# A stack of graph layers on one core: one of eight gather slots of the attention read densely on TensorE, the leaky relu's linear part added by VectorE

## The reference, cut to what matters

```python
def _gatv2(x, src, dst, Wl, Wr, att, bias):
    xl = (x @ Wl).reshape(-1, H, C)
    xr = (x @ Wr).reshape(-1, H, C)
    e = jax.nn.leaky_relu(xl[src] + xr[dst], 0.2)
    logits = jnp.einsum('ehc,hc->eh', e, att)
    m = jax.ops.segment_max(logits, dst, num_segments=N_NODES)
    p = jnp.exp(logits - m[dst])
    denom = jax.ops.segment_sum(p, dst, num_segments=N_NODES)
    alpha = p / denom[dst]
    out = jax.ops.segment_sum(alpha[:, :, None] * xl[src], dst, num_segments=N_NODES)
    return out.mean(axis=1) + bias
```

## Time and profile before

| What | Value |
|---|---|
| Median of 3 runs | 6472.8 us (6467.22 to 6487.99) |
| Profiled execution: its time | 6470.45 us |
| Its span, first to last instruction | 6468.7 us |
| PE busy | 5462.8 us, 84%, 47565 matmuls |
| PE weight loads | 3535.7 us, 55% |
| DVE busy | 3216.3 us, 50% |
| ACT busy | 1959.8 us, 30% |
| POOL busy | 4227.3 us, 65% |
| Mean granted clock of PE | 0.92 of full speed |
| DMA | 626.97 MB, mean 97 GB/s |
| Chain that ended last, by engine | PE 40%, POOL 29%, issue 15%, DVE 9% |

### The profile page before, as it was taken

The page is one execution under the profiler, slowest core; times in us unless marked ns, Lnnn a source line. Parts: engine busy times, 40 slices in busy tenths (PEclk is TensorE's granted clock), DMA queues, the critical chain, the costliest instruction groups (busy, mean ns, idle before and its releaser), DMA issues.

```text
span 6468.7 us, 138175 instructions
## 1 busy us (share of the span) xinstructions
PE 5462.8 (84%) x47565; PEld 3535.7 (55%) x47565; DVE 3216.3 (50%) x5767; ACT 1959.8 (30%) x3916; POOL 4227.3 (65%) x4383
## 2 busy tenths in 40 slices
PE   1888888868886888689999986899999679999995
PEld 1666666667775777535455544354444444455553
DVE  8222323266567555535555555355555624555555
ACT  0333334345551000033333321333333123333330
POOL 0777777657775777477777742777777147777770
PEclk8899989879997999789999996999999879999997
DMA  1444444323332332234444431444444224444441
GB/s 36 113 114 113 113 113 113 102 72 83 78 83 66 83 83 77 54 87 119 117 121 121 120 94 38 104 120 117 121 121 118 65 56 116 120 119 121 119 117 32
DMA packets 645340, 626.97 MB, mean 97 GB/s; under 512 B 366244, under 2 KB 447915, under 8 KB 644779
## 3 DMA queue, kind: packets, MB, share of 16 engines
q1 hardware_dynamic: 498218, 437.16, 22.1%
q0 software_dynamic: 140352, 181.29, 14.6%
q10 hardware_dynamic: 6208, 1.37, 0.1%
HBM read 530.77 MB, written 88.55 MB: 96 GB/s over the span
## 4 chain that ended last, share of the span: by engine, by line
PE 40%; POOL 29%; issue 15%; DVE 9%; ACT 2%; DMA 2%; DVEq 1%; POOLq 0%
POOL rows L340 29%; PE ps L761 11%; PE ps L877 10%; PE ps L848 4%; PE ps L776 4%; PE ps L865 2%; PE ps L856 2%; DMA rows<-table,idx 2%; DVE region L1326 1%; DVE acc L1442 1%; PE ps L947 1%; PE ps L833 1%; PE ps L788 1%; DVE region L1034 1%; PE ps L963 1%
## 5 line engine op out<-in xcount | busy, mean ns | idle before, releaser
L340 POOL DMA_INDIRECT rows<-table,idx x3328 | 3231.9, 971 | 1556.8 <-issue 1108.3
L877 PE MATMUL ps<-region,hot 128*128 128x272 f32 x4992 | 1320.0, 408 | 92.2 <-DVE acc L1442 87.9
L877 PEld LDWEIGHTS ps<-region,hot 128*128 128x128 f32 x4992 | 910.9, 192 | 507.9 <-issue 335.8
L573 ACT ACTIVATE region<-ps 128x512 f32<-128x512 f32 x1248 | 677.4, 595 | 1681.9 <-PE ps L848 1681.9
L1442 DVE TENSOR_TENSOR acc<-acc,ps 128x272 f32 x1248 | 545.2, 437 | 1195.6 <-PE ps L877 1088.5
L1432 DVE TENSOR_TENSOR region<-ps,region 128x1056 f32<-128x1056 f32 x624 | 781.7, 1253 | 64.8 <-issue 53.7
L761 PE MATMUL ps<-hot,region 128*128 128x192 bf16 (+1 forms) x7488 | 773.0, 266 | 13.2 <-issue 9.6
L848 PE MATMUL ps<-xT,wcat 64*128 64x512 f32 x2496 | 721.9, 655 | 7.4 <-ACT region L573 4.9
L761 PEld LDWEIGHTS ps<-hot,region 128*128 128x128 bf16 x7488 | 701.9, 105 | 40.8 <-issue 9.9
L352 POOL DMA_INDIRECT rows<-table,idx x528 | 502.6, 952 | 270.5 <-issue 160.3
L865 PE MATMUL ps<-region,attblk 128*32 128x512 f32 x2496 | 667.5, 614 | 0.0
(11 more groups left out here) (264 smaller groups left out, 5880.0 us busy)
## 6 DMA issues: line engine op xcount, KB each, us to landing
hot<-hot_dram SPq DMA_DIRECT2D x624, 256.0 KB
turned<-turned_dram SPq DMA_DIRECT2D x624, 128.0 KB
rows<-table,idx POOLq DMA_INDIRECT x3856
hot_dram<-hot SPq DMA_DIRECT2D x104, 512.0 KB
xwin<-table SPq DMA_DIRECT2D x1664, 24.0 KB
region<-hot_dram SPq DMA_DIRECT2D x78, 512.0 KB
turned_dram<-turned SPq DMA_DIRECT2D x104, 256.0 KB
region<-r_dram SPq DMA_DIRECT2D x78, 256.0 KB
```

The costliest lines, as they stand in the source:

```text
L340: pool.indirect_dma_start(rows[:, b, j, :], None, table, bass.IndirectOffsetOnAxis(ap=idx[:, s:s + 1], axis=0)).then_inc(gathered[b], 16)
L573: act.activation(rz[:, 2 * t + side, :], ps[:, Z + side, :], ACT.Relu).then_inc(rz_made, 1)
L877: mm = pe.matmul(ps[:, AG + i, 0:PC + H], hot[:, b, 4 * side + 2 * i + j, :], px[b][:, 4 * side + 2 * i + j, :], start=(j == 0), stop=(j = ...
```

## The change

1. *One slot of eight.* POOL gathers the first seven slots of a group. The eighth (side 1, j = 3) is read densely: SP's `numbers_for` loads a chunk's eight source numbers, broadcast, one DMA a chunk; DVE's `stationary_one` makes the four one-hot matrices of eight slots at once (four instructions a chunk, in phases 3 and 4); PE's `read_one(u + 2)` runs 12 bf16 matmuls into the free columns 272 to 495 of the first sums bank, behind `z_half(u, 0)`; DVE's `pick_one(u + 2)` multiplies by a mask and sums the candidates into `xs`, two instructions; `rows_in` turns that slot by one float32 matmul in place of three bf16 ones.
2. *The linear part.* `linear` and `linblk` go. ACT's relu scales by 0.8, and DVE's new `leaky` computes rz = 0.2 z + rz for 128x1024 values, reading z from PSUM, twice a step. `z_half` and the logits now wait for DVE.
3. *The logits.* All four products of a group are issued together at the step's end, each into 32 output partitions of its own; within a chunk the partitions are now ordered by head, then by group. The flags, the maxima's tiles (`exchange` copies in four parts), `fall` and `fdiag` (64 rows) follow this order.
4. *New orders and waits.* DVE in an ordinary step: `weigh` side 0, `leaky` 0, `weigh` side 1, `add` side 0, pick, `leaky` 1, `add` side 1. `rows_in` waits for the pick. `sums_half(k, 1)` waits for the pick of u + 2, since both use one bank. `read_one` waits for the adds of k - 1.
5. *Layer start.* The table's bf16 parts are copied to `tabC`, and the four masks of the first chunk are made. The self products are summed in seven parts inside the loop of 25 (four windows each), no longer by one instruction behind it. DVE's first two picks follow the clearing of `acc`.
6. *Before the attention.* `linblk`, the sums of weights that filled it and the scaling of `attblk` go; the masks `spanhot` of the runs of 512 nodes (13 small comparisons) and `headsel` are added; the flags are spread by 16 instructions of half the size.

```diff
@@ pool_gathers @@
-                slots = range(8 * g, 8 * g + 8) if pas == 0 else piece_slots(g)
+                slots = range(8 * g, 8 * g + 8) if pas == 0 else piece_slots(g)[0:7]
@@ sp_attention @@
+            def numbers_for(c):
+                if c >= CHUNKS:
+                    return
+                at = l * CHUNKS + c
+                if at >= 2:
+                    sp.wait_ge(bt1_made, FOLD * (at - 1))
+                first = CHUNK * c + CHUNK // 2 + PIECE - 1
+                sp.dma_start(rline1[at % 2].rearrange("p (n e) -> p n e", n=8),
+                             r_dram.rearrange("a (f e) -> (a f) e", f=2)[first:first + 29:4, :].partition_broadcast(P)
+                             ).then_inc(r1_in[at % 2], 16)
...
             for u in range(G + LAG):
+                if u % 8 == 5:
+                    numbers_for(u // 8 + 2)
@@ act_attention @@
                 for side in range(2):
-                    act.activation(rz[:, 2 * t + side, :], ps[:, Z + side, :], ACT.Relu).then_inc(rz_made, 1)
+                    act.activation(rz[:, 2 * t + side, :], ps[:, Z + side, :], ACT.Relu, scale=0.8).then_inc(relu_made, 1)
@@ pe_attention @@
+            def logits(g):
                 n = g % 8
+                pe.wait_ge(rz_made, 2 * (l * G + g) + 2)
...
+                for side in range(2):
+                    for t in range(2):
+                        q = 64 * side + 32 * t
+                        pe.matmul(ps[q:q + 32, LG, :], attblk[l][:, t, 7 - n:7 - n + 32], rz[:, 2 * t + side, :],
+                                  start=(n == 0), stop=(n == 7), skip_group_check=True).then_inc(l_summed, 1)
+
+            def read_one(g):
...
+                pe.wait_ge(bt1_made, FOLD * (at + 1))
+                if l * G + g > 0:
+                    pe.wait_ge(one_picked, l * G + g)
+                for k in range(FOLD):
+                    cols = len(range(k, W, FOLD)) * C
+                    for s in range(3):
+                        mm = pe.matmul(ps[:, AG, 272:272 + cols], bt1[at % 2][:, k, n, :],
+                                       tabC[:, k::FOLD, s * C:(s + 1) * C], start=(k == 0 and s == 0),
+                                       stop=(k == FOLD - 1 and s == 2), skip_group_check=True)
+                mm.then_inc(one_read, 1)
...
                 pe.wait_ge(att_added, 4 * (l * G + k) + 2 * side)
+                if side == 1 or k + LAG + 2 >= G:
+                    pe.wait_ge(one_picked, l * G + min(k + LAG + 3, G))
...
                 if u < G:
                     z_half(u, 0)
+                if u + 2 < G:
+                    if k > 0:
+                        pe.wait_ge(att_added, 4 * (l * G + k))
+                    read_one(u + 2)
...
                 if u < G:
-                    linear(u)
                     z_half(u, 1)
-                    logits_half(u, 0)
...
                 if u < G:
-                    logits_half(u, 1)
+                    logits(u)
@@ vector @@
+            def stationary_one(l, c, k):
...
+                v.tensor_scalar(bt1[at % 2][:, k, :, :].rearrange("p n e -> p (n e)"), rline1[at % 2], lanes[:, k:k + 1],
+                                None, ALU.is_equal).then_inc(bt1_made, 1)
+
+            def pick_one(l, g):
...
+                v.tensor_tensor(cand, ps[:, AG, 272:272 + GROUPS * C].rearrange("p (g c) -> p g c", g=GROUPS),
+                                wide(spanhot[:, g, :], C), ALU.mult).then_inc(one_picked, 1)
+                v.wait_ge(one_picked, at + 1)
+                v.tensor_reduce(xs[:, (g // 8) % 2, g % 8, 7, 0:C], cand.rearrange("p g c -> p c g"), AX.X, ALU.add
+                                ).then_inc(one_kept, 1)
...
+                def leaky(g, t):
...
+                    v.wait_ge(relu_made, 4 * (l * G + g) + 2 * t + 2)
+                    to = rz[:, 2 * t:2 * t + 2, :]
+                    v.scalar_tensor_tensor(to, ps[:, Z:Z + 2, :], 0.2, to, ALU.mult, ALU.add).then_inc(rz_made, 1)
...
                     link(scan_ahead(c, carrycol[:, 0:1]))
+                    leaky(u, 0)
                     link(scan_back(c, carrycol[:, 1:2]))
...
                     if phase == 0 and ends:
                         if k + 1 >= 0 and k + 1 < G:
                             weigh(k + 1, 0)
+                        leaky(u, 0)
                         v.wait_ge(lg_copied, l * CHUNKS + c + 1)
                         link(scan_ahead(c, -BIG))
                         scan_back(c, -BIG).then_inc(heads_made, 1)
                         if windows:
                             add(k, 0, windows)
+                        pick()
                         if 0 <= k + 1 < G:
                             weigh(k + 1, 1)
+                        leaky(u, 1)
                         exchange(c)
...
             for l in range(LAYERS):
                 give_table(X[:, :, :])
                 v.sem_inc(small_asked, 1)
+                v.tensor_copy(tabC, tabparts[:, :, 2 * C:5 * C]).then_inc(tab_kept, 1)
+                attention_begins(l)
```

More of the change, by code:

```diff
@@ L276, in build @@
         r_made, r_stored = sem("r_made"), sem("r_stored")
+        r1_in = [sem(f"r1_in{b}") for b in range(2)]
+        bt1_made, one_read, one_picked, one_kept = sem("bt1_made"), sem("one_read"), sem("one_picked"), sem("one_kept")
+        tab_kept = sem("tab_kept")
         r_in = [sem(f"r_in{b}") for b in range(2)]
@@ L893, in pe_attention @@
                     pe.wait_ge(endmax_copied, at + 1)
[L894 removed]
+                    pe.matmul(ps[:, MISC, 0:H], ones[0:8 * H, :], fdiag[:, :], start=True, stop=True).then_inc(fall_spread, 1)
                 if u < G:
[L896 removed]
                     z_half(u, 1)
[L898 removed]
                 if u + 1 < G:
@@ L1207, in _ @@
             cp(grp, slint)
+            ones_of = grp.rearrange("p (c a n j) -> p c a n j", c=CHUNKS, a=2, n=8)[:, :, 1, :, PIECE - 1]
+            for c in range(CHUNKS):
+                tt(spanhot[:, 8 * c:8 * c + 8, :], wide(ones_of[:, c, :], GROUPS), down(iota[:, 0:GROUPS], 8), ALU.is_equal)
             for k in range(FOLD):
@@ L1498, in attention, with pick @@
                         link(v.tensor_tensor(at, at, fscale[:, :].unsqueeze(2).broadcast_to([P, H, HK]), ALU.mult))
+                    def pick():
+                        if u + 2 < G:
+                            pick_one(l, u + 2)
+                    if phase in (3, 4) and u // 8 + 1 < CHUNKS:
+                        for q in range(2):
+                            stationary_one(l, u // 8 + 1, 2 * (phase - 3) + q)
                     if phase == 0 and ends:
@@ L1524, in attention @@
                             weigh(k + 1, 0)
+                        leaky(u, 0)
+                        if 0 <= k + 1 < G:
+                            weigh(k + 1, 1)
                         if windows:
                             add(k, 0, windows)
-                        if 0 <= k + 1 < G:
-                            weigh(k + 1, 1)
+                        pick()
+                        leaky(u, 1)
                         if windows:
```

146 lines of the change are left out of this document (86 added, 60 removed).

## The result

The kernel after takes 6707.38 us (median; 6706.54 to 6712.41), the kernel before 6470.52 in the same comparison: the ratio is 1.0362 (95% interval 1.0343 to 1.0382), so the change costs 237 us. Timed again among the experiments (e11) it was 1.038 (1.0361 to 1.04).

A forecast was written before the change was run, and what follows sets the result against it. POOL's gathers set the 10.25 us step, PE 0.5 behind; after the change DVE's queue at chunk ends costs time. +69 - 51 + 63 + 20 + 36 - 3 = +134 gives 6605 us; range 6420 to 6730.

The forecast's parts named there:

- PE in an ordinary step: The five steps of a chunk away from its end: 8.9 us on PE plus 0.15 waiting for the pick, 9.03.
- Step 0: First step behind a chunk's end, with scans, leaky and exchange queued on DVE: 13.5 us.
- Step 2: Third step behind a chunk's end: 13.8 us with 4.15 of PE idle before second z, plus 1.75 for lower clock.
- Step 1: Second step behind a chunk's end: second sums wait for the pick at 8.0, 11.6 us in all, plus 0.5 of clock.
- First 16 steps of a layer: Few sums run and POOL sets the pace: 1 us less each, -17 a layer, -51 in all.
- Layer start: First z waits for the first pick, queued on DVE: +12 us a layer, +36 in all, bounds 8 and 15.
- The last ten steps: End of each layer, with neither gathers nor logits: forecast to stay as they are.
- three terms of the sum: +69 for 33 settled chunks (84.1 against 82.0), +63 for step 2's clock, +20 for the clock in steps 0 and 1.
- DVE's idle time would take in the leaky product: Rival: leaky and pick fit DVE's idle time at the chunk's end too, chunk 78.8, total 6350 us; chance 0.15.
- The clock staying up: Rival: PE's gap in step 2 doesn't lower the clock, -83, total 6522 us; chance 0.17.
- DVE's share in the settled stretch: Sign: the prediction is wrong if DVE's share in a settled stretch is under 80%.
- the logits overlap only in pairs: Rival: the four logit products overlap only in pairs, +0.95 a step, +246, total 6850 us; chance 0.08.

The follow-up runs named there:

- e11: The kernel after, unchanged, timed again beside the kernel before in a later job: 6715.08 us, ratio 1.038.
- e4: Kernel after plus 19 matmuls with unread results behind the fall product, filling PE's gap in step 2: 6689.8 us, ratio 1.0336.
- e12: e8 plus two changes of order, in a layer's last ten steps and at its start: 6372.17 us, 0.9853 of the kernel before.
- e1: Kernel after with the linear part back as a PE matmul and no leaky on DVE, dense read kept: 6614.94 us, ratio 1.0223.
- e3: Kernel after with the fall product moved ahead of the dense read and first sums in step 2: 6587.91 us, ratio 1.0175.
- e10: e9 plus four orders (carries later, weighings ahead, last ten steps' adds, layer start), on a slower chip: ratio 0.9808 to the kernel before.
- e9: The same kernel as e8, run again on another slow chip: ratio 0.9807 to the kernel before.
- e8: Kernel after with e3's order and the linear part as a PE matmul in each chunk's first three steps, slower chip: ratio 0.9793.

## Why the prediction was right, and where its sizes were off

The direction, the mechanism and the range held (6707 in 6420 to 6730); the forecast of 6605 was 102 low, and 6707 lies 7 above 6530 to 6700, the range of the likeliest case, which had 0.53. Step by step:

- *PE in an ordinary step.* Forecast 9.03, measured 9.3. The four logit products do run at once: 4573.06 to 4574.05 in the timeline below, 0.99 us for the 1.05 I took. The Trainium skill ("TensorEngine Tiling (Array Packing)", Key Properties) says that different tiles run matmuls in parallel; this trace agrees for four float32 tiles of 128x32. The read is 1.04 (forecast 1.03). What I had too small is the wait for the pick, 0.28 for 0.15, and rows in with 0.90 (4569.87 to 4570.77) for 0.80: +0.27 x 5 = 1.35 a chunk.

```profile
4564.75 1.13 PE L879 MATMUL ps<-xT,wcat 64*128 64x512 f32 x4
4565.81 1.20 PE L903 MATMUL ps<-region 128*128 128x224 bf16 x12
4566.85 2.03 PE L919 MATMUL ps<-region,hot 128*128 128x272 f32 x8
4568.81 1.13 PE L879 MATMUL ps<-xT,wcat 64*128 64x512 f32 x4
...
4571.05 2.07 PE L919 MATMUL ps<-region,hot 128*128 128x272 f32 x8 [0.28 <-issue]
4573.06 1.07 PE L890 MATMUL ps<-region,attblk 128*32 128x512 f32 x8
4574.05 0.70 PE L879 MATMUL ps<-xT,wcat 64*128 64x512 f32 x2
```

- *DVE's prices.* Leaky 1.22 (1.22), pick 0.38 and 0.55 (0.39 and 0.53), masks 0.50 (0.515): right.
- *Step 0:* 13.5 forecast, 13.4 measured. *Step 2:* a gap of 4.15 forecast, 4.13 measured; with the clock 15.55 forecast, 15.0 measured. I had priced the clock behind it by the earlier trace rows, 1.75; from the second z to the next step the kernel after needs 6.49 us where an ordinary step needs 5.24 (4568.81 to 4574.05), 1.25, and e4 shows 0.8 of it coming back.
- *Step 1* is the term that failed most: 11.6 and 0.5 of clock forecast, 13.8 measured. There are two parts to it. The larger is VectorE's queue. At 12 of the 33 chunk ends of the kernel after, the clock is full until the second sums, as in this one, whose step begins at 3202.54 (the sums in PE's timeline, then the pick in DVE's):

```profile
3211.78 3.68 PE L919 MATMUL ps<-region,hot 128*128 128x272 f32 x8 [1.27 <-DVE region L1479]
```

```profile
3211.25 0.38 DVE L1479 TENSOR_TENSOR region<-ps,spanhot 128x224 f32<-128x224 f32 x1
```

  The pick starts 8.7 us into the step and the sums that wait for it 9.24, for the 8.0 that I had laid out: the carries' copy comes 0.4 later, DVE stands 0.69 before the second adds, and I had left out the pick's own 0.38 and its hand-over. With the 3.6 us that I had for the rest at full clock this makes 12.8, an estimate, as no step 1 of this kernel runs at full clock throughout. What is left to the clock is then 1.0 on the mean of the 33, for 0.5 forecast. I had seen that shorter gaps may lower it but took it for hidden in slack. At 21 ends it falls in the first half of the step, as at the one shown above, whose windows view over z and read (4.2 us) has half the clock; the first half then takes 5.9 to 7.0 us for 4.45, the step 12.8 to 13.9. At the other 12 it falls only at the sums (3.68 above for 2.07), and the step takes 14.4 to 14.7.

```profile
4615.30:4619.50 4.20, 2.08 (x4) 0.51 (x4) 0.50 0.44 111
```

- *First 16 steps of a layer:* -17 forecast, -13 measured (145.3 for 158.3). *Layer start:* +12 forecast, +10.9 measured (44.7 us from the table's last cast to the first z, 33.8 before). *The last ten steps* "stay": wrong, +6.2 a layer (90.0 from the last step's z to the last add, 83.8 before). `weigh` of side 1 now stands in front of the adds of side 0 even where no leaky product follows; e12, which exchanges them there, takes 82.1.
- Together: the settled chunks cost 33 x 6.8 = 224 for the 152 of three terms of the sum (69, 63 and 20), +72; first steps +12, drain +18, starts -3, the saving before the attention, which didn't show, +3: the 102 that were missing.
- *The rivals.* That DVE's idle time would take in the leaky product (6350) fell at the point that it named: leaky of step 2 starts 7.2 us into the step, not before 5. The clock staying up (6522) fell too. Of my own tests, one went against its letter: DVE's share in the settled stretch is 690.45 / 888.6 = 78%, under the 80% that I had set; with the chunk of 86.3 us that I had forecast, clock included, it would have been 80%. The rival by which the logits overlap only in pairs (6850) fell too: 0.99 us for all four.
- What I hadn't seen is that the largest single item came from the order of two lists more than from the load of an engine. I costed the fall product's wait rightly, but as a price of the leaky product. e1 has it without leaky, e3 removes it with leaky in place, and of the 237 us it was 120.

## What to carry to other kernels

In lists written out by hand, a small product that one engine makes for the other belongs ahead of every long one that doesn't need it: each side's queue stands behind it, and work added in front of it delays both. Where an engine has idle time only on average, move work to it by place: the linear part on VectorE pays in the five steps where TensorE sets the pace and costs in the three where VectorE's chain does; e12, with it only in the five, has both. Price a gap of TensorE by its length and by the clock of what follows it: removing the wait of 4.13 us gave 120 us, filling it 17.

## What was not expected of the hardware

Behind stands of TensorE of 0.93, 0.70 and 1.74 us, with 2.1 and 1.1 us of matmuls between them, the granted clock was 0.50 for 4.2 us; the kernel before had at most one stretch of the lower level in the last 11 chunks of a layer, e12 none. Here z, read and sums went from 4.06 to 6.92 us (4615.35 to 4622.27). At 12 of the 33 chunk ends the same stands left these three at full clock, and the clock fell behind the next two, of 0.9 and 1.3 us. The Trainium skill ("TensorE: Matmul & The Clock Gate", A second HAM failure mode) describes such short idling between groups of matmuls, and a clock that goes back and forth by it, for bf16 products that cycle through PSUM banks; this trace agrees for float32 products behind waits on VectorE.

Two jobs of four had the kernel before 30% slower (8409 and 8440 for 6471 us), and all traces from there have some 400 stands of TensorE, of up to 1.2 us, inside rows of matmuls that wait for no semaphore. That TensorE waited for its own instructions there is only argued from the fact that the profile names nothing else. On such a chip e10, with four orders more than e9, was no faster, and ratios from there don't carry over: e8 had 0.979 and 0.981 on them, while e12, which has two gains more, had 0.985 elsewhere.
